# One maximum instruction over two PSUM banks, with four banks for the maxima and two for the scores

## The chip, the cores and the metric

The kernel runs on one core of one Trainium2 chip. The metric is the time of one execution on the device, in microseconds. TensorE (PE) multiplies matrices and writes into PSUM, an accumulation memory of eight banks of 2 KB in each partition; VectorE (DVE), ScalarE (ACT) and GpSimd (POOL) do the elementwise work, and SyncE (SP) issues the transfers. The engines run beside each other and meet only at semaphores.

## The reference

One decoder layer over 32 batches of 56 tokens and 128 channels, in three parts, each with a residual and a layer norm behind it: causal self-attention with one head, cross-attention with 16 heads of 8 channels over a context of 1500 rows, and a gated feed-forward part.

```python
x = _layernorm(x + attn(x))                       # self-attention, 56 tokens
# cross-attention
q, k, v = shape(x @ wq), shape(ctx @ wk), shape(ctx @ wv)      # 16 heads of 8
scores  = einsum('bhtd,bhsd->bhts', q, k) + bias               # 56 x 1500 for each head
attn    = einsum('bhts,bhsd->bhtd', softmax(scores), v)
x = _layernorm(x + attn @ wo)
x = _layernorm(x + ffn(x))
```

The bias depends on the distance between token and context row, and is constant beyond some distance.

## The kernel before, in words

Three blocks follow each other: self-attention, cross-attention, feed-forward. The change touches cross-attention, which takes from about 113 to 840 us of the span.

**Batches and steps.** `iteration(g, u)` treats one batch of the 32, in 12 steps `j` (`ST = 12`), one for each 128 of the 1500 context rows. Every engine runs the same loop with its own program, and nothing but semaphores orders them. Two more iterations ahead of the first batch only prepare.

**Scores.** In step `j` TensorE makes the scores of one context tile for all heads, context rows on the partitions, in two halves of eight heads (`scores`, h = 0 and 1; 4 matmuls each, line 610). Each half fills 448 columns of one bank of `st_ps`. Half number w goes into bank `w % ST_BANKS`, and TensorE first waits until ScalarE has done the exponential of half w - `ST_BANKS` (semaphore `s_ex`). ScalarE turns each half into `e_sb` (line 811). In steps 0 and 1 VectorE adds the near bias to the scores in place before that (line 719).

**Maxima.** The softmax needs the maximum of each row ahead of the exponential, so the scores of the next batch are made once more in the other layout, tokens on the partitions: 24 chunks (8 head pairs times 3 ranges of context), each one matmul of up to 512 columns into one bank of `max_ps` (`max_chunk`, line 113). VectorE reduces each chunk to one column of `cmax`: chunks 0 to 7 (c = 0, the range near the tokens, with the bias added) with the instruction of line 120, chunks 8 to 23 with the plain maximum of line 123. Two chunks belong to each step: steps 8 to 11 make chunks 0 to 7 of the batch after next, steps 0 to 7 chunks 8 to 23 of the next batch. TensorE waits for the maximum of chunk n - `MAX_BANKS` (`s_mr`). After chunk 23 VectorE combines `cmax`, splits the negated maximum into three bfloat16 parts (lines 731 to 740, "the nm chain"), TensorE transposes them (line 668, step 9), ScalarE copies them (line 802) and a transfer puts them into `qst` for the next batch's scores.

**What stands between.** TensorE's order in a step is: scores half 0, scores half 1, first chunk, [transposed maxima in step 9], in odd steps the product of weights and values for two tiles (`pv_ps`, lines 640 and 649), second chunk, and then the step's user of the bank `misc`: values of the context in steps 10, 0 and 1 (line 691), the denominators in step 3 (lines 697, 698), keys in steps 4, 5 and 7 (line 686). ScalarE's order in a step is: exponential of half 0, [`k_left` or `kpart` copies of the step before], exponential of half 1, other copies from `misc`. The key copies (line 784 `kpart`, line 793 `k_left`) for the products of steps 5 and 7 are both late (`LATE_K = (5, 7)`): they stand between the two exponentials of steps 6 and 8. Batches 0 to 28 prepare keys for the batch three ahead (`later(g, u + 3)`); the last three have none to prepare.

```python
ST_BANKS, MAX_BANKS = 3, 3
LATE_K = (5, 7)
```

Of the kernel before, what the change touches and what calls it, by code (L numbers as in the profile page):

```python
# [20 lines left out]
ALU = mybir.AluOpType  # L21
ACT = mybir.ActivationFunctionType
AX = mybir.AxisListType
# [10 lines left out]
TT = 2 * T  # L34
# [14 lines left out]
BOUND = (0, S - 2 * 512, S - 512, S)  # L49
# [10 lines left out]
A_COLS, B_COLS = 3 * T, 2 * T  # L60
PIECES = 5
E_RING = 4
ST_BANKS, MAX_BANKS = 3, 3
MASKED = -10000000000.0
LOWEST = -3.0e38
TWO_ONES = float(np.array([0x3F803F80], np.uint32).view(np.float32)[0])
# [50 lines left out]
def reduce_scores(nc, m, src, r, c, p):  # L117

    if c == 0:
        return nc.vector.tensor_tensor_reduce(  # L120
            out=m.near_out[:, p % MAX_BANKS, :], in0=src[0:TT, 0:FIRST_CH], in1=m.near_nat[:, p, :],
            scale=1.0, scalar=LOWEST, op0=ALU.add, op1=ALU.max, accum_out=m.cmax[:, r, 0, p:p + 1])
    return nc.vector.tensor_reduce(m.cmax[:, r, c, p:p + 1], src[0:TT, 0:BOUND[c + 1] - BOUND[c]], AX.X, ALU.max)  # L123


def self_attention_block(nc, d, m):
# [369 lines left out]
def cross_attention_block(nc, d, m):  # L496

    with ExitStack() as ctx:
# [8 lines left out]
        max_ps = ctx.enter_context(nc.psum_tensor("max_ps", [P, MAX_BANKS, 512], F32))  # L507
# [10 lines left out]
        s_mx, s_mr = m.s_mx, m.s_mr  # L518
# [11 lines left out]
        def batch(g, u):  # L530
            return BODY * g + u

        def run(iteration):

            def whole(eng):
                for b in range(FIRST, B + 1):
                    iteration(0, b)
            return whole
# [9 lines left out]
        def wait(eng, s, v):  # L548
            if not isinstance(v, int) or v > 0:
                eng.wait_ge(s, v)  # L550

        def live(g, n):

            return not isinstance(g, int) or 0 <= n < B
# [8 lines left out]
        CHUNKS = PAIRS * NCH  # L563
# [7 lines left out]
        def max_items(g, u, j):  # L571

            for i in range(2):
                lag, n = (1, 2 * (j + ST - M0) + i) if j < M0 else (2, 2 * (j - M0) + i)
                if live(g, u + lag):
                    yield lag, n, n // PAIRS, n % PAIRS
# [126 lines left out]
        @block.vector  # L703
        def _(dve):
            def iteration(g, u):
                b = batch(g, u)
                for j in range(ST):
                    if j < 2 and live(g, u):
                        for h in range(2):
                            w = 2 * (b * ST + j) + h  # L710
                            dve.wait_ge(s_st, w + 1)
                            if j == 0:
                                t, near = st_ps[:, w % ST_BANKS, 0:HALF], m.near_t0[:, h * HALF:(h + 1) * HALF]
                            else:
                                t = st_ps[0:NEAR - P, w % ST_BANKS, 0:HALF].rearrange("p (h t) -> p h t", t=T)
                                t = t[:, :, T - NEAR + P:T]
                                near = m.near_t1[:, h * HALF:(h + 1) * HALF].rearrange("p (h t) -> p h t", t=T)
                                near = near[:, :, T - NEAR + P:T]
                            nc.vector.tensor_tensor(t, t, near, ALU.add).then_inc(s_nb, 1)  # L719
                    if j == XH and live(g, u - 1):  # L720
                        dve.wait_ge(s_ro, b)
                        dve.wait_ge(s_rc, 2 * b)
                        nc.vector.tensor_tensor(rec[:, :], x_own[:, :], rec[:, :], ALU.mult).then_inc(s_xo, 1)
                    for lag, n, c, p in max_items(g, u, j):
                        dve.wait_ge(s_mx, (b + lag) * CHUNKS + n + 1)
                        reduce_scores(nc, m, max_ps[:, n % MAX_BANKS, :], (u + lag) % 2, c, p).then_inc(s_mr, 1)
                    if j == NM and live(g, u + 1):
                        dve.wait_ge(s_mr, (b + 2) * CHUNKS)
                        wait(dve, s_nt, b + 1)
                        wait(dve, s_nm, b + 1)  # L730
                        nc.vector.tensor_reduce(nm_ps[0:TT, 0, :], m.cmax[:, (u + 1) % 2, :, :].rearrange("q c p -> q p c"),
                                                AX.X, ALU.max, negate=True).then_inc(s_n0, 1)
                        dve.wait_ge(s_n0, b + 2)
                        nc.vector.tensor_copy(nm3[:, 0, :], nm_ps[0:TT, 0, :]).then_inc(s_n1, 1)
                        dve.wait_ge(s_n1, 2 * b + 3)
                        nc.vector.tensor_tensor(nm_ps[0:TT, 1, :], nm_ps[0:TT, 0, :], nm3[:, 0, :], ALU.subtract).then_inc(s_n1, 1)
                        dve.wait_ge(s_n1, 2 * b + 4)
                        nc.vector.tensor_copy(nm3[:, 1, :], nm_ps[0:TT, 1, :]).then_inc(s_n2, 1)
                        dve.wait_ge(s_n2, b + 2)
                        nc.vector.tensor_tensor(nm3[:, 2, :], nm_ps[0:TT, 1, :], nm3[:, 1, :], ALU.subtract).then_inc(s_nm, 1)  # L740
                    if live(g, u - 1):
                        if j == REC_A:
                            dve.wait_ge(s_dr, b)
                            wait(dve, s_xh, 2 * (b - 1))
                            nc.vector.reciprocal(rec[:, 0:A_COLS], den[:, 0:A_COLS]).then_inc(s_rc, 1)
                        if j == REC_B:
                            nc.vector.reciprocal(rec[:, A_COLS:A_COLS + B_COLS],
                                                 den[:, A_COLS:A_COLS + B_COLS]).then_inc(s_rc, 1)
                        if j == XH:
                            dve.wait_ge(s_xo, b)  # L750
                            for i, (lo, hi) in enumerate(((0, A_COLS), (A_COLS, A_COLS + B_COLS))):
                                nc.vector.tensor_reduce(m.xh[:, i, bass.ds((b - 1) * T, T)],
                                                        rec[:, lo:hi].rearrange("p (i t) -> p t i", t=T),
                                                        AX.X, ALU.add).then_inc(s_xh, 1)

            run(iteration)(dve)

        @block.scalar
# [510 lines left out]
```

## Time and profile before

| | |
|---|---|
| median of 3 runs | 1002.92 us (1002.01 to 1007.84) |
| the profiled execution | 1000.81 us, of which the span in the trace is 999.0 us |
| PE busy | 925.6 us (93%) |
| DVE busy | 729.5 us (73%) |
| ACT busy | 608.3 us (61%) |
| POOL busy | 376.1 us (38%) |

Busy time is the time in which an engine works on something; matmuls overlap each other in the array, so that PE's busy time is an upper estimate. Between the span and the execution's own time lie 1.8 us at the ends.

### The profile page before, as it was taken

What the parts mean: (1) busy time and instruction counts of PE and PEld (TensorE: products, weight loads), DVE (VectorE), ACT (ScalarE), POOL (GpSimd) and SP (SyncE); (2) the same over time, 40 slices, a digit from 0 to 9 for tenths busy, and PEclk for the clock granted to TensorE, in tenths of its full rate; (3) what the DMA queues carried; (4) which work ended last, traced back from release to release, by engine and by line L of the source; (5) the groups of instructions that cost most, each with busy time, mean ns of one, the idle gap of its engine ahead of it and who ended that gap; (6) DMA issues with size and microseconds to landing.
All of it is one profiled execution on the core that took longest, in us unless ns stands there. A gap on an engine that the chain in (4) does not pass through costs nothing. (4 is left out here: it accounts for less than half of the span.)

```text
span 999.0 us, 26082 instructions
## 1 busy us (share of the span) xinstructions
PE 925.6 (93%) x10410; PEld 650.3 (65%) x10410; DVE 729.5 (73%) x1705; ACT 608.3 (61%) x1423; POOL 376.1 (38%) x317
## 2 busy tenths in 40 slices
PE   6876799999999999999999999999999987999996
PEld 3653477767777777777677777677776666555564
DVE  5567678888888888888888888888888873610023
ACT  2242477777777777777777677777777664632232
POOL 7300445555544444455555444444555200000000
PEclk9777799999999999999999999999999998999999
DMA  7739766656667767666666676676665502100001
GB/s 206 260 84 162 214 183 184 179 179 192 194 195 202 199 197 201 192 205 181 178 194 194 186 203 197 202 196 200 188 199 148 148 2 61 60 1 0 1 10 28
DMA packets 56324, 154.96 MB, mean 155 GB/s; under 512 B 23234, under 2 KB 35322, under 8 KB 53114
## 3 DMA queue, kind: packets, MB, share of 16 engines
q1 hardware_dynamic: 55820, 152.44, 53.4%
q8 instruction: 82, 1.34, 0.6%
q10 hardware_dynamic: 384, 0.86, 0.3%
q14 instruction: 38, 0.31, 0.1%
HBM read 110.03 MB, written 42.63 MB: 153 GB/s over the span
## 5 line engine op out<-in xcount | busy, mean ns | idle before, releaser
L811 ACT ACTIVATE e_sb<-st_ps 128x448 f32<-128x448 f32 (+1 forms) x768 | 382.9, 556 | 127.1 <-PE st_ps L610 66.2
L123 DVE TENSOR_REDUCE cmax<-max_ps 112x1 f32<-112x512 f32 x512 | 330.8, 680 | 56.3 <-PE max_ps L113 56.0
L113 PE MATMUL max_ps<-kst,qst 111*112 111x512 bf16 (+1 forms) x768 | 268.0, 390 | 6.1 <-PEq L132 3.1
L610 PEld LDWEIGHTS st_ps<-qst,kst 114*128 114x128 bf16 (+1 forms) x3072 | 194.7, 101 | 105.1 <-ACT e_sb L811 36.1
L610 PE MATMUL st_ps<-qst,kst 114*128 114x112 bf16 (+1 forms) x3072 | 229.5, 213 | 15.9 <-ACT e_sb L811 11.8
L120 DVE CUSTOM_DVE_ANT_0 near_out<-max_ps,near_nat 112x476 bf16<-112x476 f32 x256 | 157.1, 650 | 36.5 <-PE max_ps L113 33.9
L851 POOL TENSOR_TENSOR kpart<-k_left,kpart 128x500 bf16<-128x500 f32 x90 | 102.0, 1134 | 204.7 <-ACT k_left L793 204.7
L640 PE MATMUL pv_ps<-e_sb,vals 128*32 128x168 f32 (+1 forms) x3072 | 149.5, 312 | 0.0
L857 POOL TENSOR_TENSOR kpart<-k_left,kpart 128x500 bf16<-128x500 f32 x90 | 125.9, 1398 | 7.1
L113 PEld LDWEIGHTS max_ps<-kst,qst 111*112 111x112 bf16 x768 | 85.5, 131 | 47.0 <-issue 20.5
L691 PEld LDWEIGHTS misc<-wv,ctxt 128*128 128x128 f32 (+1 forms) x768 | 101.4, 191 | 8.1 <-issue 1.2
L640 PEld LDWEIGHTS pv_ps<-e_sb,vals 128*32 128x32 f32 (+1 forms) x3072 | 80.5, 109 | 39.8 <-issue 20.0
L854 POOL TENSOR_TENSOR k_left<-k_left,kpart 128x500 f32<-128x500 f32 x90 | 102.2, 1136 | 7.1
L691 PE MATMUL misc<-wv,ctxt 128*128 128x128 f32 (+1 forms) x768 | 102.7, 277 | 0.4 <-ACT vals L770 0.4
L686 PE MATMUL misc<-ctxt,wk 128*128 128x500 f32 x180 | 90.4, 583 | 0.8 <-ACT k_left L793 0.8
L865 POOL TENSOR_TENSOR x_own<-x_sb,own 128x280 f32<-128x280 f32 x32 | 21.0, 655 | 184.8 <-ACT x_sb L820 184.8
L1138 DVE TENSOR_TENSOR y<-ff_ps,s 112x512 f32<-112x512 f32 x4 | 2.8, 690 | 97.2 <-PE ff_ps L1036 97.2
L649 PE MATMUL pv_ps<-e_sb,vals 128*32 128x112 f32 (+1 forms) x1536 | 72.1, 259 | 0.0
L768 ACT COPY vals<-misc 128x384 f32<-128x384 f32 (+2 forms) x128 | 51.2, 400 | 33.3 <-PE misc L691 33.3
L784 ACT CAST kpart<-misc 128x500 bf16<-128x500 f32 x90 | 51.5, 572 | 16.4 <-PE misc L686 16.4
L719 DVE TENSOR_TENSOR st_ps<-st_ps,near_t 18x144 f32<-18x144 f32 (+1 forms) x128 | 53.4, 460 | 8.4 <-PE st_ps L610 8.4
L793 ACT COPY k_left<-misc 128x500 f32<-128x500 f32 x90 | 53.2, 591 | 0.0
(126 smaller groups left out, 893.1 us busy)
## 6 DMA issues: line engine op xcount, KB each, us to landing
kst<-kparts SPq DMA_DIRECT2D x192, 375.0 KB, 6.8
kparts<-kpart SPq DMA_DIRECT2D x90, 375.0 KB, 2.7
ctxt<-in_ctxT SPq DMA_DIRECT2D x31, 750.0 KB, 7.9
qst<-qslots SPq DMA_DIRECT2D x192, 28.0 KB, 7.1
qslots<-qst SPq DMA_DIRECT2D x4, 672.0 KB, 10.2
kparts<-kst SPq DMA_DIRECT2D x6, 375.0 KB, 3.2
h<-in_h SPq DMA_DIRECT2D x2, 1024.0 KB, 7.3
qslots<-kst SPq DMA_DIRECT2D x24, 56.0 KB, 4.5
```

Source lines behind the costliest of these rows:

```text
L113: return nc.tensor.matmul(dst[0:TT, 0:hi - lo], m.qst[0:M_ROW, r, p, :], m.kst[0:M_ROW, r, p, lo:hi], start=True, stop=True)
L120: return nc.vector.tensor_tensor_reduce(out=m.near_out[:, p % MAX_BANKS, :], in0=src[0:TT, 0:FIRST_CH], in1=m.near_nat[:, p, :], scale=1.0 ...
L123: return nc.vector.tensor_reduce(m.cmax[:, r, c, p:p + 1], src[0:TT, 0:BOUND[c + 1] - BOUND[c]], AX.X, ALU.max)
L610: mm = nc.tensor.matmul(st_ps[0:K, w % ST_BANKS, p * TT:(p + 1) * TT], m.kst[0:AUG, u % RING, 4 * h + p, j * P:j * P + K], m.qst[0:AUG, u ...
L640: nc.tensor.matmul(pv_ps[32 * q:32 * q + 32, 0:A_COLS], m.vals[0:K, u % 2, j, 32 * q:32 * q + 32], e_sb[0:K, j % E_RING, q * A_COLS:(q + 1 ...
L649: mm = nc.tensor.matmul(pv_ps[32 * q:32 * q + 32, A_COLS:A_COLS + B_COLS], m.vals[0:K, u % 2, j, 32 * (4 + i):32 * (5 + i)], e_sb[0:K, j % ...
L686: nc.tensor.matmul(misc[:, 0:CH], wk[:, :], ctxt[:, r, part * CH:(part + 1) * CH], start=True, stop=True).then_inc(s_kp, 1)
L691: mm = nc.tensor.matmul(misc[0:st_rows(t), i * C:(i + 1) * C], ctxt[:, r, t * P:t * P + st_rows(t)], wv[:, :], start=True, stop=True)
L811: nc.scalar.activation(e_sb[0:K, j % E_RING, h * HALF:(h + 1) * HALF], st_ps[0:K, w % ST_BANKS, 0:HALF], ACT.Exp).then_inc(s_ex, 1)
L851: nc.gpsimd.tensor_tensor(kpart[:, 1, cols], k_left[:, cols], kpart[:, 0, cols], ALU.subtract).then_inc(s_kr, 1)
L854: nc.gpsimd.tensor_tensor(k_left[:, cols], k_left[:, cols], kpart[:, 0, cols], ALU.subtract).then_inc(s_kr, 1)
L857: nc.gpsimd.tensor_tensor(kpart[:, 2, cols], k_left[:, cols], kpart[:, 1, cols], ALU.subtract).then_inc(s_k3, 1)
```

## The change

The eight PSUM banks are dealt out anew: `max_ps` gets four instead of three, `st_ps` two instead of three, and `pv_ps` and `misc` keep one each. With `ST_BANKS = 2`, half w of the scores waits for the exponential of half w - 2, which is the same half of the step before. With `MAX_BANKS = 4`, a chunk waits for the maximum of the chunk four before it. For chunks 8 to 23 VectorE waits until both chunks of a step are there and takes the two maxima with one instruction, that reads two neighbouring banks (112 x 2 x 512) and writes two columns of `cmax`; it adds 2 to `s_mr`. Chunks 0 to 7 stay as they are.

```diff
-ST_BANKS, MAX_BANKS = 3, 3
+ST_BANKS, MAX_BANKS = 2, 4
@@ reduce_scores
-    return nc.vector.tensor_reduce(m.cmax[:, r, c, p:p + 1], src[0:TT, 0:BOUND[c + 1] - BOUND[c]], AX.X, ALU.max)
+    return nc.vector.tensor_reduce(m.cmax[:, r, c, p:p + 2], src[0:TT, :, 0:BOUND[c + 1] - BOUND[c]], AX.X, ALU.max)
@@ cross_attention_block, vector
                     for lag, n, c, p in max_items(g, u, j):
-                        dve.wait_ge(s_mx, (b + lag) * CHUNKS + n + 1)
-                        reduce_scores(nc, m, max_ps[:, n % MAX_BANKS, :], (u + lag) % 2, c, p).then_inc(s_mr, 1)
+                        if c == 0:
+                            dve.wait_ge(s_mx, (b + lag) * CHUNKS + n + 1)
+                            reduce_scores(nc, m, max_ps[:, n % MAX_BANKS, :], (u + lag) % 2, c, p).then_inc(s_mr, 1)
+                        elif n % 2 == 0:
+                            first = n % MAX_BANKS
+                            dve.wait_ge(s_mx, (b + lag) * CHUNKS + n + 2)
+                            reduce_scores(nc, m, max_ps[:, first:first + 2, :], (u + lag) % 2, c, p).then_inc(s_mr, 2)
```

On VectorE this is the order in steps 0 to 7 of a batch before (near bias of the scores, chunks 8 to 23, and the reciprocals of the denominators):

```order
L719 TENSOR_TENSOR st_ps<-st_ps,near_t 128x448 [waits ca_st] x2
L123 TENSOR_REDUCE cmax<-max_ps 112x1 [waits mx] x2
L719 TENSOR_TENSOR st_ps<-st_ps,near_t 18x8x18 [waits ca_st] x2
L123 TENSOR_REDUCE cmax<-max_ps 112x1 [waits mx] x8
L745 RECIPROCAL rec<-den 128x168 [waits ca_xh,ca_dr]
L123 TENSOR_REDUCE cmax<-max_ps 112x1 [waits mx] x2
L747 RECIPROCAL rec<-den 128x112
```

And the same stretch of the changed kernel (lines below the change stand five lower):

```order
L719 TENSOR_TENSOR st_ps<-st_ps,near_t 128x448 [waits ca_st] x2
L123 TENSOR_REDUCE cmax<-max_ps 112x2 [waits mx]
L719 TENSOR_TENSOR st_ps<-st_ps,near_t 18x8x18 [waits ca_st] x2
L123 TENSOR_REDUCE cmax<-max_ps 112x2 [waits mx] x4
L750 RECIPROCAL rec<-den 128x168 [waits ca_dr]
L123 TENSOR_REDUCE cmax<-max_ps 112x2 [waits mx]
L752 RECIPROCAL rec<-den 128x112
```

Each two maxima of one column have become one of two columns, in the same place.

On ScalarE the order stays as it was; in steps 6, 7 and 8 (and the start of step 9) it reads, in both kernels but for the line numbers:

```order
L811 ACTIVATE e_sb<-st_ps 128x448 [waits ca_st,ca_pv]
L784 CAST kpart<-misc 128x500 [waits ca_k3,ca_kp]
L793 COPY k_left<-misc 128x500
L811 ACTIVATE e_sb<-st_ps 128x448 [waits ca_st]
L811 ACTIVATE e_sb<-st_ps 128x448 [waits ca_st,ca_pv]
L811 ACTIVATE e_sb<-st_ps 128x448 [waits ca_st]
L811 ACTIVATE e_sb<-st_ps 128x448 [waits ca_st,ca_pv]
L784 CAST kpart<-misc 128x500 [waits ca_k3,ca_kp]
L793 COPY k_left<-misc 128x500
L811 ACTIVATE e_sb<-st_ps 128x448 [waits ca_st]
L802 CAST nmp<-misc 24x112 [waits ca_md1,ca_nt]
```

Nothing has moved here; what changed is which of these exponentials a half of the scores waits for.

## Rows read from the trace of the kernel before

**Rows 1.** Busy time of each engine by stretch (us; PEclk: granted clock)

```profile
core 0: us, PE busy (x) PEld busy (x) DVE busy (x) ACT busy (x) POOL busy (x), PEclk, DMA share, GB/s
480.84:503.77 22.93, 22.29 (x301) 16.29 (x300) 19.92 (x46) 16.76 (x41) 11.63 (x11) 1.00 0.66 195
136.59:822.30 685.71, 662.92 (x8950) 484.87 (x8948) 592.78 (x1366) 496.64 (x1216) 327.11 (x282) 1.00 0.64 185
0.00:100.00 100.00, 72.60 (x372) 49.02 (x372) 64.81 (x129) 29.17 (x60) 27.35 (x14) 0.81 0.71 178
800.00:830.00 30.00, 25.80 (x432) 19.43 (x430) 19.61 (x42) 20.86 (x51) 1.31 (x2) 1.00 0.01 2
```

**Rows 2.** Waits in 136.59 to 822.3 us: in total us, times, longest

```profile
PEld st_ps L610 <- ACT e_sb L811: 31.8, 118, 0.5
...
PEld max_ps L113 <- DVE cmax L120: 10.2, 58, 0.4
...
PEld max_ps L113 <- DVE cmax L123: 7.0, 35, 0.6
...
PE max_ps L113 <- DVE cmax L123: 0.5, 2, 0.3
```

**Rows 3.** Groups of VectorE in batch 16, 480.84 to 503.77 us

```profile
L123 DVE TENSOR_REDUCE cmax<-max_ps 112x1 f32<-112x512 f32 x16 | 10.4, 680 | 1.7 <-PE max_ps L113 1.7
...
L731 DVE TENSOR_REDUCE pv_ps<-cmax 112x8 f32<-112x24 f32 x1 | 0.2, 189 | 0.0
```

**Rows 4.** ScalarE in batch 16, timeline: start, us, what

```profile
482.33 1.02 ACT L811 ACTIVATE e_sb<-st_ps 128x448 f32<-128x448 f32 x2 [1.61 <-DVE st_ps L719]
...
485.69 0.40 ACT L768 COPY vals<-misc 128x288 f32<-128x288 f32 x1 [0.17 <-PE misc L691]
...
486.32 1.87 ACT L811 ACTIVATE e_sb<-st_ps 128x448 f32<-128x448 f32 x4
...
493.96 0.54 ACT L811 ACTIVATE e_sb<-st_ps 128x448 f32<-128x448 f32 x1 [1.03 <-PE st_ps L610]
494.40 0.57 ACT L784 CAST kpart<-misc 128x500 bf16<-128x500 f32 x1
494.85 0.60 ACT L793 COPY k_left<-misc 128x500 f32<-128x500 f32 x1
495.32 1.45 ACT L811 ACTIVATE e_sb<-st_ps 128x448 f32<-128x448 f32 x3
...
498.90 0.58 ACT L811 ACTIVATE e_sb<-st_ps 128x448 f32<-128x448 f32 x1
...
499.48 0.96 ACT L811 ACTIVATE e_sb<-st_ps 128x448 f32<-128x448 f32 x2
```

**Rows 5.** TensorE in batch 16, timeline

```profile
483.13 0.38 PE L113 MATMUL max_ps<-kst,qst 111*112 111x512 bf16 x1
...
484.61 1.05 PE L691 MATMUL misc<-wv,ctxt 128*128 128x128 f32 x8
...
486.95 0.37 PE L610 MATMUL st_ps<-qst,kst 114*128 114x112 bf16 x4 [0.27 <-ACT e_sb L811]
487.16 0.38 PE L113 MATMUL max_ps<-kst,qst 111*112 111x512 bf16 x1
...
493.50 0.56 PE L610 MATMUL st_ps<-qst,kst 114*128 114x112 bf16 x8
...
494.77 0.38 PE L113 MATMUL max_ps<-kst,qst 111*112 111x512 bf16 x1
495.08 0.78 PE L640 MATMUL pv_ps<-e_sb,vals 128*32 128x168 f32 x16
...
497.08 0.56 PE L610 MATMUL st_ps<-qst,kst 114*128 114x112 bf16 x8
...
498.34 0.37 PE L113 MATMUL max_ps<-kst,qst 111*112 111x476 bf16 x1
499.08 0.22 PE L668 MATMUL misc<-ident_b,nm 112*24 112x112 bf16 x1 [0.37 <-ACT k_left L793]
499.09 0.78 PE L640 MATMUL pv_ps<-e_sb,vals 128*32 128x168 f32 x16
```

## The prediction

> **What bounds the kernel now.** I read the busy time by stretch first, to find the engine that sets the pace; then the waits of that engine; then one batch in order of time, with the two engines that the change couples more tightly. From 136.59 to 822.30 us thirty batches pass, 22.86 us each, and PE is busy for 662.92 of 685.71 us, 97% [rows 1]. PE sets the pace, and all that could be won by taking waits away from it is 22.8 us. VectorE is busy 86% there and ScalarE 72%. The waits say who holds PE up: its weight loads wait 31.8 us for exponentials (the third bank of `st_ps` not yet free), and 10.2 + 7.0 us for maxima; but matmuls are still under way during most of these, for PE itself stands still behind a plain maximum only 0.5 us in thirty batches [rows 2]. So the maxima hardly slow PE, and the exponentials already do, with three banks.
>
> **The maxima: what goes.** Per batch, 16 maxima of line 123 become 8. Now they take 10.4 us of VectorE, 680 ns each alone [rows 3]. No row shows a maximum over two banks. Upper bound: twice one, 1.36 us. Lower bound: 24 elements take 189 ns and 512 take 680 ns [rows 3], so an element costs (680 - 189) / 488 = 1.0 ns, and 1024 take 0.68 + 0.51 = 1.19 us. I take 1.19, the lower end, as the slope comes from the same operation. Eight cost 9.5 to 10.9 against 10.4 us: between 0.9 won and 0.5 lost per batch, on an engine that is not the bound. At either end PE gains at most its waits for maxima, 0.5 to 17.7 us in thirty batches [rows 2]; I take 0, since PE's own row has 0.5.
>
> **The maxima: what is added.** VectorE now waits for the second chunk of a step before it takes either. Behind that wait stand, on VectorE, the near bias of step 1, the reciprocals and the nm chain. The last is the one that somebody waits for: PE transposes its result at 499.08, and that instruction waits today for `k_left` and not for VectorE [rows 5]. The chain would end at most one maximum (0.68) minus the saved part later, about 0.5 us; and PE will come to this place about 3 us later, as shown next. Cost: 0; if the cover were gone, 0.5 us per batch. On PE's side chunk n waits for chunk n - 4, two steps back: 0.
>
> The Trainium skill (Trace Analysis, Optimizing Scalar/DVE Operations) has a rule against this half of the change: where VectorE or ScalarE is not saturated but causes bubbles on another engine, instructions are better broken up than joined. The rows have VectorE at 86% and PE itself hardly held by it [rows 1, 2], so the rule's condition is not met here; by the rule the 0.5 us of the nm chain would be paid, and the sum would come out 30 x 0.5 = 15 us higher, 1116.
>
> **The scores: the new waits.** Half h of step j now waits for the exponential of half h of step j - 1. I replay batch 16 with the durations of its own rows. A half starts 0.06 us after the exponential that it waited for: today one at 486.95 behind an exponential that ends at 486.32 + 0.57 [rows 4, 5]. The first chunk follows the second half by 0.20 us (486.95 to 487.16), and an exponential starts 0.46 us after its half on an idle ScalarE (493.50 to 493.96), ends 0.57 later, and the next follows it by 0.43 (four in 1.87 us) [rows 4, 5]. Four places have to wait:
>
> 1. Step 0 to 1. The two exponentials of step 0, late because of the near bias, end at 482.33 + 1.02 = 483.35. Half 1 of step 1 starts at 483.41, the chunk behind it at 483.61 in place of 483.13: **+0.48** [rows 4, 5].
> 2. Step 2 to 3. ScalarE first copies the values of step 1: the product starts at 484.61, now 485.09; the copies start 1.08 later and take 0.63 (485.69 to 486.32), so that step 2's exponentials start at 486.80 and 487.23 and the second ends at 487.80. The chunk comes at 487.80 + 0.26 = 488.06 in place of 487.16: +0.90, of which **+0.42** is new [rows 4, 5].
> 3. Step 6 to 7. Half 0 of step 6 starts at 493.50 + 0.90 = 494.40. Then the chain on ScalarE: exponential (+0.46), `kpart` (+0.44), `k_left` (+0.45), exponential of half 1 (+0.47), its end (+0.58): 496.80. Chunk at 497.06 in place of 494.77: +2.29, **+1.39** new [rows 4, 5]. PE has only two halves and two chunks to do meanwhile.
> 4. Step 8 to 9. The same chain from half 0 of step 8, 497.08 + 2.29 = 499.37: 2.40 + 0.26 later the chunk, at 502.03 in place of 498.34, +3.69. But today PE then waits for `k_left` until 499.08; now `k_left` ended long before. The values product follows its chunk by 0.31, as in step 7 (494.77 to 495.08): 502.34 in place of 499.09, +3.25, **+0.96** new [rows 4, 5].
>
> At the other steps the exponential is done in time: behind odd steps PE has a values product of about 0.9 us and a `misc` product. The closest is step 9 to 10. Its exponentials end 1.36 us after the transposed maxima start (499.08 to 500.44), in the new time at about 503.6, just when the half wants to start (500.24 today plus 3.25, plus 0.20): no wait, or one of a tenth. Sum: 0.48 + 0.42 + 1.39 + 0.96 = **3.25 us per batch**.
>
> 29 batches prepare keys: 29 x 3.25 = 94.3. The last three keep places 1 and 2, 0.9 each; without key products between, their even steps come closer together, at most as much again: 2.7 to 5.4, from which VectorE's relief may take 1. I take 3.5. Sum: +98 us on the 1000.81 us of the profiled execution, 1098.8; the median of the runs lies 2.1 higher, so **1101 us**.
>
> **The range of the sum.** If place 1 or 2 is absorbed: -0.45 per batch; if step 9 to 10 and each restart cost 0.1 more: +0.5. Thirty batches: 1087 to 1116; rounded to 1084 to 1118 this is the forecast, chance 0.79.
>
> **Rivals.**
> - *Only the late keys cost.* If the exponentials of steps 0 and 2 come earlier, as VectorE reaches the near bias sooner, only places 3 and 4 are paid: 29 x 2.35 = 68, 1071 us. For it: VectorE gains up to 0.9 us a batch. Against: the near bias stands in front of the first pair. Chance 0.08.
> - *Every wait is paid in full*, with none absorbed (place 4 keeps its 0.44, restarts of PE cost more than the 0.06 seen): 4 to 5 us per batch, 29 x 4.5 + 5 = 135, 1138 us. For: PE restarts four times instead of once. Against: today's one restart costs nothing beyond. Chance 0.08.
> - *The clock falls.* The granted clock is 1.00 in the loop, and 0.81, a mix of 2.4 and 1.2 GHz, in the first 100 us, in which PE is busy 73% [rows 1]. The new loop has PE busy for 22.3 of 26.2 us, 85%, with gaps up to 1.4 us. Against: 800 to 830 us has 86% at 1.00 [rows 1]. At 0.81 the 22.3 us would become 27.5: +5.2 x 30 more, about 1255 us. The Trainium skill (TensorE: Matmul & The Clock Gate, A second HAM failure mode: psum-queue depth-cycling) describes just this, a kernel that cycles through PSUM banks and idles briefly between groups, whose clock swings. Chance 0.03.
> - *Not slower.* VectorE is what PE waits for, through the weight loads: its relief gives back up to 17.7 us [rows 2], and the two banks suffice. This needs step 6's second exponential to be done when half 1 of step 7 wants to start, 494.57, and it starts at 495.32 [rows 4]; it decides only if PE arrives there over a microsecond later for another reason. 985 to 1003 us, chance 0.02.
>
> **How the numbers follow.** The predicted time is the forecast's, 1101. Forecast alone leaves 0.21 out; the range reaches a little towards both neighbours, 1080 to 1122. A measurement of this kernel can tell about 1% from no change; faster by over 1%: 0.01; within: 0.01; slower: 0.98.
>
> **What the profile after would show.** The batches start 26.2 us apart; the waits name `st_ps` behind `e_sb`, for PE itself, as the longest of PE, with single waits of 1 to 1.4 us; the gaps stand between the halves of steps 7 and 9, and smaller ones in steps 1 and 3; the transposed maxima wait for nobody; VectorE's maxima take about 9.5 us in a batch and its share falls below 80% in the loop; the clock is 1.00. I would be wrong if PE could pass these halves earlier than ScalarE's order lets it, which needs an order of ScalarE other than read, or if the clock fell.

## The result, and the profile after

The changed kernel takes 1105.63 us (median; 1104.61 to 1108.3) against 1002.46 us: a ratio of 1.1029, 95% interval 1.100 to 1.1058. It is 10% slower; 1101 us were forecast, 1080 to 1122 the range.

The busy time by stretch, for batch 16 and for batches 1 to 29, with the columns of [rows 1]:

```profile
534.68:560.95 26.27, 23.21 (x301) 16.08 (x299) 19.58 (x38) 17.11 (x41) 11.04 (x10) 1.00 0.57 170
140.45:899.59 759.14, 671.08 (x8666) 465.22 (x8665) 567.51 (x1102) 493.70 (x1183) 310.09 (x281) 1.00 0.57 166
```

A batch takes 26.27 us and took 22.93 [rows 1]. The clock is 1.00 still, and the number of matmuls is the same. VectorE is busy a little less (19.58 against 19.92 us); TensorE is busy 0.92 us more (23.21 against 22.29) and idle 3.06 us where it was idle 0.64. The two changes on TensorE (0.92 and 2.42) make the 3.34 us; why its busy time grew with the same matmuls is taken up in the last section. Whom TensorE waited for, in the kernel before in the stretch of [rows 1] and [rows 2] (the two longest):

```profile
PE misc L668 <- ACT k_left L793: 10.4, 28, 0.4
PE st_ps L610 <- ACT e_sb L811: 9.0, 34, 0.3
```

And in the changed kernel, in batches 1 to 29 (these are all that the view has of PE itself):

```profile
PE st_ps L610 <- ACT e_sb L816: 77.5, 115, 1.0
PE misc L668 <- DVE nm L745: 0.7, 1, 0.7
```

The wait of the scores for exponentials (`st_ps` behind `e_sb`) went from 9.0 us in thirty batches to 77.5 us in twenty-nine. No wait for a maximum is among them, and the transposed maxima no longer wait for `k_left`. VectorE's maxima in batch 16, the counterpart of [rows 3]:

```profile
L123 DVE TENSOR_REDUCE cmax<-max_ps 112x2 f32<-112x1024 f32 x8 | 9.7, 1215 | 5.0 <-PE max_ps L113 4.9
```

Eight of 1215 ns instead of sixteen of 680 ns; busy 9.7 us in place of 10.4. The 0.7 us saved have become idle time: VectorE now waits 4.9 us for chunks where it waited 1.7.

TensorE in batch 16 in order of time, the counterpart of [rows 5]:

```profile
534.68 0.56 PE L610 MATMUL st_ps<-qst,kst 114*128 114x112 bf16 x8
...
537.46 0.38 PE L113 MATMUL max_ps<-kst,qst 111*112 111x512 bf16 x1
...
541.92 0.38 PE L113 MATMUL max_ps<-kst,qst 111*112 111x512 bf16 x1
...
548.26 0.56 PE L610 MATMUL st_ps<-qst,kst 114*128 114x112 bf16 x8
548.66 0.60 PE L113 MATMUL max_ps<-kst,qst 111*112 111x512 bf16 x2
549.32 0.37 PE L610 MATMUL st_ps<-qst,kst 114*128 114x112 bf16 x4
550.72 0.37 PE L610 MATMUL st_ps<-qst,kst 114*128 114x112 bf16 x4 [1.02 <-ACT e_sb L816]
550.92 0.38 PE L113 MATMUL max_ps<-kst,qst 111*112 111x512 bf16 x1
...
553.24 0.56 PE L610 MATMUL st_ps<-qst,kst 114*128 114x112 bf16 x8
...
554.29 0.37 PE L610 MATMUL st_ps<-qst,kst 114*128 114x112 bf16 x4
555.69 0.37 PE L610 MATMUL st_ps<-qst,kst 114*128 114x112 bf16 x4 [1.02 <-ACT e_sb L816]
555.89 0.37 PE L113 MATMUL max_ps<-kst,qst 111*112 111x476 bf16 x1
556.19 0.22 PE L668 MATMUL misc<-ident_b,nm 112*24 112x112 bf16 x1
556.20 0.78 PE L640 MATMUL pv_ps<-e_sb,vals 128*32 128x168 f32 x16
...
557.35 0.63 PE L610 MATMUL st_ps<-qst,kst 114*128 114x112 bf16 x8
```

And ScalarE beside it:

```profile
548.72 0.54 ACT L816 ACTIVATE e_sb<-st_ps 128x448 f32<-128x448 f32 x1 [1.03 <-PE st_ps L610]
549.16 0.57 ACT L789 CAST kpart<-misc 128x500 bf16<-128x500 f32 x1
549.62 0.59 ACT L798 COPY k_left<-misc 128x500 f32<-128x500 f32 x1
550.08 1.58 ACT L816 ACTIVATE e_sb<-st_ps 128x448 f32<-128x448 f32 x3
```

The two largest gaps stand between half 0 and half 1 of steps 7 (549.32 to 550.72) and 9 (554.29 to 555.69). Half 1 of step 7 starts at 550.72, as the second exponential of step 6, which began at 550.08 and takes 0.58, ends at 550.66; two key copies stood ahead of it. ScalarE is busy 17.11 of 26.27 us: not its load holds TensorE, but the order in which it does its work.

### The profile page after: what moved, and what is told of

The parts are those of the page before. It is cut to its first block and busy times, and to the rows that moved or that the text cites. A ratio compares the mean times of both kernels' runs of the same rounds, so it can differ in the third digit from the quotient of the medians.

```text
span 1103.5 us, 26082 instructions
## 1 busy us (share of the span) xinstructions
PE 951.2 (86%) x10410; PEld 640.9 (58%) x10410; DVE 718.5 (65%) x1449; ACT 620.2 (56%) x1423; POOL 359.8 (33%) x317
## 5 line engine op out<-in xcount | busy, mean ns | idle before, releaser
L816 ACT ACTIVATE e_sb<-st_ps 128x448 f32<-128x448 f32 (+1 forms) x768 | 390.4, 550 | 168.1 <-PE st_ps L610 104.1
L123 DVE TENSOR_REDUCE cmax<-max_ps 112x2 f32<-112x1024 f32 x256 | 310.6, 1216 | 154.6 <-PE max_ps L113 151.4
L610 PE MATMUL st_ps<-qst,kst 114*128 114x112 bf16 (+1 forms) x3072 | 241.7, 214 | 102.3 <-ACT e_sb L816 85.1
L610 PEld LDWEIGHTS st_ps<-qst,kst 114*128 114x128 bf16 (+1 forms) x3072 | 183.7, 100 | 230.1 <-ACT e_sb L816 180.6
L113 PE MATMUL max_ps<-kst,qst 111*112 111x512 bf16 (+1 forms) x768 | 265.3, 389 | 4.6 <-PEq L132 3.2
L856 POOL TENSOR_TENSOR kpart<-k_left,kpart 128x500 bf16<-128x500 f32 x90 | 108.3, 1203 | 252.0 <-ACT k_left L798 252.0
L862 POOL TENSOR_TENSOR kpart<-k_left,kpart 128x500 bf16<-128x500 f32 x90 | 102.1, 1134 | 7.1
L719 DVE TENSOR_TENSOR st_ps<-st_ps,near_t 18x144 f32<-18x144 f32 (+1 forms) x128 | 53.6, 460 | 10.4 <-PE st_ps L610 10.3
```

Source lines behind the costliest of these rows:

```text
L113: return nc.tensor.matmul(dst[0:TT, 0:hi - lo], m.qst[0:M_ROW, r, p, :], m.kst[0:M_ROW, r, p, lo:hi], start=True, stop=True)
L123: return nc.vector.tensor_reduce(m.cmax[:, r, c, p:p + 2], src[0:TT, :, 0:BOUND[c + 1] - BOUND[c]], AX.X, ALU.max)
L610: mm = nc.tensor.matmul(st_ps[0:K, w % ST_BANKS, p * TT:(p + 1) * TT], m.kst[0:AUG, u % RING, 4 * h + p, j * P:j * P + K], m.qst[0:AUG, u ...
L816: nc.scalar.activation(e_sb[0:K, j % E_RING, h * HALF:(h + 1) * HALF], st_ps[0:K, w % ST_BANKS, 0:HALF], ACT.Exp).then_inc(s_ex, 1)
L856: nc.gpsimd.tensor_tensor(kpart[:, 1, cols], k_left[:, cols], kpart[:, 0, cols], ALU.subtract).then_inc(s_kr, 1)
L862: nc.gpsimd.tensor_tensor(kpart[:, 2, cols], k_left[:, cols], kpart[:, 1, cols], ALU.subtract).then_inc(s_k3, 1)
```

## The experiments

For each, the stretch of the 28 batches from the second to the 29th is compared, which all prepare keys; its length by 28 is the time of a batch. A single batch of the steady loop is a little shorter (22.93 us before, 26.27 after): in most kernels here two of the 28 take 0.2 to 0.3 us more. The ratio compares medians of whole runs with the kernel before as it ran beside them (median 1003.8 us for e1 to e4, 1005.5 for e5 to e8, 1004.8 for e9 and e10).

| kernel | 28 batches, us | one batch | ratio to before, 95% interval |
|---|---|---|---|
| before | 642.63 | 22.95 | |
| after | 735.99 | 26.29 | 1.1029 (1.100 to 1.1058) |
| e1: two and four banks, single maxima | 735.86 | 26.28 | 1.0997 (1.0945 to 1.1048) |
| e2: two and three banks, single maxima | 735.90 | 26.28 | 1.0999 (1.0942 to 1.1056) |
| e3: after, exponentials before late keys | 694.50 | 24.80 | 1.059 (1.0541 to 1.0639) |
| e4: after, no late keys | 721.13 | 25.76 | 1.0845 (1.0798 to 1.0891) |
| e5: before, transposed maxima behind values | 633.34 | 22.62 | 0.9906 (0.9878 to 0.9934) |
| e6: before, exponentials before late keys | 655.08 | 23.40 | 1.013 (1.0105 to 1.0156) |
| e7: before, both edits | 635.39 | 22.69 | 0.9941 (0.9917 to 0.9964) |
| e8: four and two banks | 682.38 | 24.37 | 1.0396 (1.0369 to 1.0424) |
| e9: after, no near bias on the scores | 717.41 | 25.62 | 1.0792 (1.075 to 1.0835) |
| e10: after, both edits | 680.67 | 24.31 | 1.0431 (1.0404 to 1.0458) |

### Which part of the change costs: e1 and e2

e1 takes the joined maxima back and keeps the banks:

```diff
 (kernel before)
-ST_BANKS, MAX_BANKS = 3, 3
+ST_BANKS, MAX_BANKS = 2, 4
```

> Two score banks and four maxima banks as in the change, but each chunk keeps its own maximum (16 instructions of 680 ns instead of 8 of 1216 ns). If the two score banks cost everything, the time stays with the changed kernel: 1105 us, within 6, and the batches start 26.3 us apart. If the joined maxima, or the wait for both chunks, hold TensorE up, the time falls clearly, to between 1002 and 1085 us.

Measured: 1105.19 us. e2 changes one number alone:

```diff
 (kernel before)
-ST_BANKS, MAX_BANKS = 3, 3
+ST_BANKS, MAX_BANKS = 2, 3
```

> One number of the kernel before is changed: two score banks in place of three, three maxima banks, single maxima, one PSUM bank unused. If the score banks cost everything, this alone gives the whole loss: 1105 us, within 6, 26.3 us per batch. If the fourth maxima bank or the joined maxima have a part in it, it comes out under 1085; if they give something back that the score banks take, over 1111.

Measured: 1106.74 us, and on TensorE the same two gaps as in the changed kernel (timeline of e2):

```profile
552.11 0.37 PE L610 MATMUL st_ps<-qst,kst 114*128 114x112 bf16 x4
553.50 0.37 PE L610 MATMUL st_ps<-qst,kst 114*128 114x112 bf16 x4 [1.02 <-ACT e_sb L811]
...
557.08 0.37 PE L610 MATMUL st_ps<-qst,kst 114*128 114x112 bf16 x4
558.47 0.37 PE L610 MATMUL st_ps<-qst,kst 114*128 114x112 bf16 x4 [1.02 <-ACT e_sb L811]
```

Taking away the third score bank is the whole loss. With two score banks, joined maxima and a fourth bank for them change the 28 batches by 0.1 us in 736. The joined maxima do save VectorE work, and this is worth nothing at the end. Whether joined maxima would be worth something beside three score banks was not tried: eight banks don't hold three, four, and the two others.

### Why two banks are dear: e3, e4, e9

e3 moves the late key copies behind both exponentials of their step:

```diff
 (changed kernel, ScalarE, loop over h)
-                            if h == 0:
+                            if h == (1 if j - 1 in LATE_K else 0):
                                 rest_of_k(g, u, j - 1)
```

> The changed kernel, with the two late key copies of steps 6 and 8 behind both exponentials of the step instead of between them. If ScalarE's order is what makes two banks dear, half 1 of steps 7 and 9 has to wait only for two exponentials in a row: its chunk comes 1.5 + 0.2 us after half 0 of the step before, against 1.27 with three banks, +0.45 instead of +1.39, and step 9 keeps some 0.45 as the transposed maxima wait for the later key copy: 1.8 us per batch instead of 3.34, 29 x 1.5 = 44 us less than the changed kernel, 1060 us. If two banks are too few whatever stands between, it stays over 1095.

Measured: 1064.63 us. The timeline of TensorE in e3, steps 8 and 9:

```profile
529.57 0.56 PE L610 MATMUL st_ps<-qst,kst 114*128 114x112 bf16 x8
...
531.26 0.37 PE L113 MATMUL max_ps<-kst,qst 111*112 111x476 bf16 x1
532.00 0.22 PE L668 MATMUL misc<-ident_b,nm 112*24 112x112 bf16 x1 [0.37 <-ACT k_left L798]
```

The chunk comes 1.69 us after half 0 of the step before (1.7 expected), where it took 2.65 in the changed kernel (553.24 to 555.89). And the wait of the transposed maxima for the second key copy is back, as expected: the edit moves part of the cost there. 41.5 us of the 93 that the 28 batches had lost return by another order of two copies and an exponential, with the same banks and the same work.

e4 takes one of the two copies out of the place:

```diff
 (changed kernel)
-        LATE_K = (5, 7)
+        LATE_K = ()
```

> The changed kernel with LATE_K empty: the first key copy of steps 5 and 7 stands at the end of its own step, and only the second (0.46 us) is left between the exponentials of steps 6 and 8. By ScalarE's order the waits at steps 7 and 9 each become shorter by 0.45, 0.9 per batch, 26 us in 29 batches: 1080 us. If the length of what stands between the two exponentials doesn't matter, 1105.

Measured: 1090 us: 0.53 us per batch less, in place of 0.9. The direction is right, the size was too large. ScalarE in e4, step 6:

```profile
540.44 0.58 ACT L789 CAST kpart<-misc 128x500 bf16<-128x500 f32 x1 [0.77 <-PE misc L686]
540.92 0.55 ACT L816 ACTIVATE e_sb<-st_ps 128x448 f32<-128x448 f32 x1
541.35 0.58 ACT L798 COPY k_left<-misc 128x500 f32<-128x500 f32 x1
541.81 1.58 ACT L816 ACTIVATE e_sb<-st_ps 128x448 f32<-128x448 f32 x3
```

and TensorE's half 0 of that step:

```profile
540.25 0.56 PE L610 MATMUL st_ps<-qst,kst 114*128 114x112 bf16 x8
```

The first copy has to wait for the key product, which TensorE finishes just before this half, and so it still stands ahead of the first exponential: that one starts 0.67 us after its half (540.25 to 540.92), and 0.46 in the changed kernel (548.26 to 548.72). Of the 0.45 us saved, 0.21 are lost there, and as much at step 8 (first exponential at 545.63, half at 544.96).

e9 tests place 1 of the prediction. It leaves the near bias out of the scores (the maxima keep it), so that the kernel no longer computes the layer; it serves to time the place:

```diff
 (changed kernel)
-                    if j < 2 and live(g, u):
+                    if False:
@@ ScalarE
-                            if j < 2:
-                                act.wait_ge(s_nb, 4 * b + 2 * j + h + 1)
```

> The changed kernel without the four near-bias additions of each batch on VectorE (the bias is left out of the scores; the maxima keep theirs), and without ScalarE's wait for them. By the replay, half 1 of step 1 waits in the changed kernel for an exponential that is late only because of these additions: it starts 2.57 us into the batch and would start at 1.92, 0.65 us earlier, and what follows with it: 25.6 us per batch, 31 x 0.65 = 20 us less, 1085 us. If the place doesn't count, because a later wait (steps 2 to 3) takes the time back, 1105.

Measured: 1086.76 us, 25.62 us per batch, 0.66 less. That is more than the 0.48 us of place 1, since half 1 of step 1 is late in the kernel before too (2.09 us into the batch, and 1.92 here). Step 1 follows its product without a gap (TensorE in e9, where the changed kernel has 534.68 to 536.77 and a wait inside the group):

```profile
527.49 0.56 PE L610 MATMUL st_ps<-qst,kst 114*128 114x112 bf16 x8
...
529.21 0.56 PE L610 MATMUL st_ps<-qst,kst 114*128 114x112 bf16 x8
529.61 0.38 PE L113 MATMUL max_ps<-kst,qst 111*112 111x512 bf16 x1
...
534.07 0.38 PE L113 MATMUL max_ps<-kst,qst 111*112 111x512 bf16 x1
```

The chunk of step 3 comes 4.46 us behind that of step 1 here (529.61 to 534.07), and as much in the changed kernel (537.46 to 541.92). So the wait at place 1 adds to that at place 2, which does not take its time back.

### The exchange the other way: e8

```diff
 (kernel before)
-ST_BANKS, MAX_BANKS = 3, 3
+ST_BANKS, MAX_BANKS = 4, 2
```

> The exchange in the other direction: four score banks and two maxima banks, single maxima. The waits of the scores in the kernel before, about 0.7 us per batch, go; a chunk now waits for the maximum of the chunk two before it, which by the rows of the kernel before ends too late by 0.3 us in steps 0, 1, 7 and 10, and by 0.95 in step 9, of which 0.5 is waited for today. Sum 1.65 - 0.7 = +0.95 us per batch: 23.9 us, 1030 us. If the score banks alone matter, it comes out at 980 us.

Measured: 1044.61 us, 24.37 us per batch; the sum had 23.9. Two rows of TensorE's waits over the whole span of e8:

```profile
PE max_ps L113 <- DVE cmax L120: 30.5, 66, 1.2
PE max_ps L113 <- DVE cmax L123: 14.8, 77, 0.6
```

and the place with the longest, step 9:

```profile
518.70 0.56 PE L610 MATMUL st_ps<-qst,kst 114*128 114x112 bf16 x8
520.04 0.41 PE L113 MATMUL max_ps<-kst,qst 111*112 111x476 bf16 x1 [0.79 <-DVE cmax L120]
```

The waits of the scores for exponentials are gone and those of the chunks for maxima have come. Step 9 costs 0.94 us (520.04 against the 519.10 at which the chunk would follow two halves of 0.20 us each), as expected. What the sum missed stands in step 3 of the same batch:

```profile
506.87 0.56 PE L610 MATMUL st_ps<-qst,kst 114*128 114x112 bf16 x8
507.60 0.42 PE L113 MATMUL max_ps<-kst,qst 111*112 111x512 bf16 x1 [0.17 <-DVE cmax L123]
```

The second half no longer waits 0.43 us for an exponential, but the chunk behind it, which would follow at 507.27, now comes early enough to wait for its maximum, until 507.60: 0.33 of the 0.43 us won are paid out again. A wait had hidden another. That explains 0.33 of the 0.47 us by which the batch is longer than the sum.

### What is left in the kernel before: e5, e6, e7, and e10

The replay named one more wait in the kernel before: the transposed maxima for the second key copy, 0.37 us in TensorE's row [rows 5]. e5 moves them:

```diff
 (kernel before, TensorE, in a step)
-                    if user and user[0] == "nmt":
-                        (transposed maxima)
+                    if user and user[0] == "nmt":
+                        pe.wait_ge(s_nm, batch(g, u + user[2]) + 1)
                     if j % 2 and live(g, pv[1]):
                         value_pair(*pv)
+                    if user and user[0] == "nmt":
+                        (transposed maxima)
@@ ScalarE: the nmp copy of step NMT from ahead of the two exponentials to behind them
```

> The kernel before (three and three banks, single maxima), with TensorE's transposed maxima of step 9 behind the values product instead of ahead of it, and ScalarE's copy of them behind the two exponentials of the step. Theory: what is left on TensorE in the kernel before is again an engine that meets ScalarE's order, the wait of 0.5 us for the second late key copy; behind the values product (0.9 us) it is gone. 0.45 us per batch less, 22.48 us apart, 29 x 0.45 = 13 us: 990 us. Rival: the transfer of the transposed maxima, which starts 0.9 us later, comes too late for the next batch's scores, and the time stays at 1003 or grows.

Measured: 996.0 us, ratio 0.9906. TensorE in step 9 of e5:

```profile
494.53 0.37 PE L113 MATMUL max_ps<-kst,qst 111*112 111x476 bf16 x1
494.83 0.78 PE L640 MATMUL pv_ps<-e_sb,vals 128*32 128x168 f32 x16
495.43 0.37 PE L649 MATMUL pv_ps<-e_sb,vals 128*32 128x112 f32 x8
495.62 0.21 PE L673 MATMUL misc<-ident_b,nm 112*24 112x112 bf16 x1
```

The values product follows its chunk by 0.30 us (0.75 before), the wait is gone, and the transfer of the transposed maxima still comes in time. That is 9.3 us in 28 batches, 0.33 each on average and 0.39 in most, where 0.45 was expected; the time came out at 996 and not 990 us. This version is the fastest here, 0.9% better than the kernel before (interval of the ratio 0.9878 to 0.9934): small, but seen in the batches as well.

e6 gives the kernel before the edit of e3:

> The kernel before, three and three banks, with the two late key copies behind both exponentials of steps 6 and 8, the edit that took 41 us off the version with two banks. With three banks half 1 of step 7 waits for the first exponential of step 6 alone, so that nothing is won there; the second key copy of step 8 ends 0.44 us later and the transposed maxima wait for it: 23.37 us per batch, 29 x 0.44 = 13 us more, 1016 us. If exponentials ahead of copies were better in itself, it would come out below 1003.

Measured: 1017.56 us, 23.40 us per batch, as expected; PE's wait for `k_left` doubles, over the whole span (10.7 us in the kernel before):

```profile
PE misc L668 <- ACT k_left L793: 22.6, 28, 0.8
```

The same edit that wins 41 us with two banks loses 12 us with three. e7 has both edits on three banks:

> Both edits on the kernel before: key copies behind the exponentials, and the transposed maxima behind the values product, where the later key copy costs nothing. As e5, 22.48 us per batch and 990 us; if the later key copy still shows, up to 1000.

Measured: 999.06 us, 22.69 us per batch. A little worse than e5: the key copy, later by 0.44 us, still shows. In one batch of e7 it ends at 497.93 on ScalarE and the transposed maxima start at 497.98, 2.44 us behind half 0 of step 8 where it is 2.35 us in e5. That makes 0.06 us in most batches; three batches also waited 0.3 to 0.9 us for a transfer (`qst` from `qslots`). e10 puts both edits on the changed kernel:

> The changed kernel with key copies behind both exponentials and the transposed maxima behind the values product. The first edit alone gave 24.79 us per batch, with TensorE again waiting about 0.4 us for the second key copy in step 9; the second edit should take that: 24.4 us per batch, 29 x 0.4 = 12 us less, 1053 us. Even so two score banks stay 5% slower than three, as the waits of steps 1, 3, 7 and 9 remain at 0.4 to 0.5 us each. If ordering alone could make two banks do, it would come near 1005.

Measured: 1048.59 us, 24.31 us per batch (24.4 expected). Order wins back 55 of the 93 us. The rest is the price of two banks whatever the order: against e7, which has the same orders and three banks, 45.3 us in 28 batches, 1.6 per batch. It stands at the four places: counted from the start of batch 16, the first chunks of steps 1, 3, 7 and 9 come at 2.78, 7.24, 15.28 and 19.29 us in e10 and at 2.30, 6.33, 13.93 and 17.51 in e7, so each place adds 0.43 to 0.48.

## Why the prediction was right

**What bounds the kernel.** Right. TensorE sets the pace before, and its wait for exponentials is the only one that grew.

**The maxima.** Right, sum 0. An instruction over two banks takes 1215 ns; 1.19 us was taken, 1.36 the other end. The second chunk's wait costs nobody here: e1 and the changed kernel agree to 0.13 us in 28 batches. Both have two score banks, which leave VectorE idle for longer; beside three no run shows it. The rule of the Trainium skill (Perfetto Trace Analysis, Optimizing Scalar/DVE Operations), by the prediction's reckoning 15 us more for the joined instruction, had nothing to act on: its condition, a VectorE that holds another engine up, is absent from TensorE's waits.

**The scores, place by place.** The chunk behind each place, counted from the start of the batch, replay against trace:

| place | before | replay | after |
|---|---|---|---|
| 1, step 1 | 2.29 | 2.77 | 2.78 |
| 2, step 3 | 6.32 | 7.22 | 7.24 |
| 3, step 7 | 13.93 | 16.22 | 16.24 |
| 4, step 9 | 17.50 | 21.19 | 21.21 |
| values product behind it | 18.25 | 21.50 | 21.52 |
| next batch | 22.93 | 26.18 | 26.27 |

(480.84 and 534.68 taken off.) Up to place 4 the replay is off by 0.02. What it left out is the close place between steps 9 and 10, "no wait, or one of a tenth": the group at 557.35 takes 0.63 and not 0.56, its second half has waited 0.07. So 3.34 us per batch in place of 3.25. e3 and e4 show that places 3 and 4 stand on ScalarE's order, for about 0.95 us each; what e10 has left there, 0.43 to 0.44 us each, comes with nothing but two exponentials in a row. e9 shows that place 1 stands on the near bias. Place 2 has no experiment of its own, only its row, 541.92, and e10 against e7.

**The sum.** From the first to the 30th batch 96.2 us have come in (666.14 to 762.34), 94.3 forecast. The last three batches took 4.95 us more (0.85, 1.65 and 2.45, the last one up to the first matmul of the feed-forward part), 3.5 forecast. These two terms were set 1.9 and 1.45 us too low. The last batch has no chunks between its scores, which leaves ScalarE less time between two halves; that this is the reason was not tried. The remaining 3.3 us of the 104.5 by which the spans differ lie outside: the first scores start at 114.10 in place of 113.08, and the feed-forward part takes 2.3 us more. The edit touches neither, and both scatter as much among the other kernels here (first scores 111.3 to 116.8 us, feed-forward part 155.8 to 160.7). So 97.8 us were forecast for the loop and 101.2 came; the other 3.3 us lie within this scatter.

**The rivals.** "Only the late keys cost" falls with e9. "Every wait in full" falls with the table: a restart of TensorE costs 0.06 us behind the exponential (550.66 to 550.72), as in the kernel before. "Not slower" falls with e1 and e2. The granted clock was 1.00, the 2.4 GHz level, over batches 1 to 29 (140.45 to 899.59 us), with TensorE busy 88% and gaps of 1.0 us; the swinging that the Trainium skill describes (TensorE: Matmul & The Clock Gate, A second HAM failure mode: psum-queue depth-cycling) was not met. PE's busy share came out at 88%, not 85%: its busy time was taken as unchanged and grew to 23.2 us (last section).

## What to carry to other kernels

The number of buffers between two engines is to be judged by how long the emptying engine takes at its latest places, not by its load: ScalarE was busy 65% here. One bank less made 0.9 us of copies between two exponentials, until then hidden, visible twice a batch, and with these copies moved away four places still cost 1.6 us a batch (e10 against e7). Before a buffer is taken from one ring for another, replay one period from the timeline with the waits it would have; on a steady loop this gave the time to 0.1 us in 26. A saving on an engine that nobody waits for (the maxima of VectorE, 0.7 us per batch) turns into idle time, and the right order of two lines depends on the number of buffers: the same edit won 41 us with two banks and lost 12 with three.

## What the runs showed that was not expected

- One maximum over two banks (1024 elements) takes 1215 ns, two over one bank 680 each: 0.14 us less for a pair. Where they follow each other closely neighbours overlap, and a batch has 9.7 us of the double ones against 10.4 of the single ones.
- TensorE's busy time per batch rose from 22.29 to 23.21 us with the same matmuls at the same clock. The matmuls did not get longer: the times of the single ones as the profile has them (several are under way at once), added up over the 28 batches, make 83.5 us per batch before and 83.6 after. What changed is how far they overlap, so here the busy time rose by stalls alone.
- In e5 a batch takes 22.54 us mostly, but two of 29 took 22.8 and two more 23.0 and 23.8. The first two stand in the kernel before as well (23.2 us, the fifth and the 19th batch). The other two each waited once for a transfer, as TensorE's waits in the 28 batches show:

```profile
PE max_ps L113 <- DMA qst<-qslots: 1.6, 2, 1.2
```

Such waits are not e5's own: in their whole spans e7 has three, 1.8 us in all, e6 one of 1.0 and the kernel before one of 0.3. Why the transfer was late in these batches stays open.
